# A graph-network kernel: 64-wide segment windows in one PSUM bank, edge values copied to PSUM by ScalarE, and another order of the last stretch

## The reference, cut to what matters

```python
# layer 0
h = gelu(x @ W_pre + b_pre)
aggr = segment_sum(h[src] * edge_attr, dst)
t = x + aggr
x = layernorm(x + t + gelu(gelu(t @ W1 + b1) @ W2 + b2))
# layer 1
norm = dinv[src] * dinv[dst]
agg = segment_sum((x @ W_lin.T + b_lin)[src] * norm[:, None], dst)
x = layernorm(x + relu(agg + x @ W_root.T + b_root))
```

## Time and profile before

| | us |
|---|---|
| median of three runs | 1217.83 (1215.64 to 1218.61) |
| the profiled execution | 1216.85 |
| its span, first to last instruction | 1215.0 |
| PE busy | 970.0 (80%) |
| POOL busy | 848.8 (70%) |
| DVE busy | 733.6 (60%) |
| ACT busy | 497.3 (41%) |

### The profile page before, as it was taken

The page is one execution under the profiler, slowest core; times in us unless marked ns, Lnnn a source line. Parts: engine busy times, 40 slices in busy tenths (PEclk is TensorE's granted clock), DMA queues, the critical chain, the costliest instruction groups (busy, mean ns, idle before and its releaser), DMA issues.

```text
span 1215.0 us, 21150 instructions
## 1 busy us (share of the span) xinstructions
PE 970.0 (80%) x7552; PEld 828.6 (68%) x7552; DVE 733.6 (60%) x1424; ACT 497.3 (41%) x820; POOL 848.8 (70%) x940
## 2 busy tenths in 40 slices
PE   6737677767768778879888989999999987996663
PEld 6635444434447557758767878899999986896553
DVE  8286867577765787676576676444455443543443
ACT  2305776565754676475655666300001000110032
POOL 7787777777777777777777777777777777760022
PEclk9767978687778889999999999999999997999766
DMA  8534776665657597888878988988888875878211
GB/s 222 160 107 130 260 234 227 195 222 179 232 188 223 184 318 250 259 263 258 274 247 283 294 291 283 311 260 231 245 228 243 222 207 148 255 189 200 70 48 42
DMA packets 195626, 263.62 MB, mean 217 GB/s; under 512 B 76828, under 2 KB 173084, under 8 KB 188540
## 3 DMA queue, kind: packets, MB, share of 16 engines
q1 hardware_dynamic: 167834, 218.28, 56.9%
q0 software_dynamic: 27392, 43.48, 14.4%
q10 hardware_dynamic: 290, 0.45, 0.1%
HBM read 175.10 MB, written 87.00 MB: 216 GB/s over the span
## 4 chain that ended last, share of the span: by engine, by line
PE 40%; POOL 32%; issue 12%; ACT 8%; DVE 5%; DMA 2%; SPq 1%; DVEq 0%; POOLq 0%; ACTq 0%
POOL gath L782 27%; PE bank_q L1393 24%; PE seg L1333 7%; ACT counts_raw L870 7%; PE bank_q L1364 5%; POOL gath L761 3%; PE bank_a L1293 1%; DMA gath<-table_h,srcs 1%; PE bank_q L1412 1%; DVE hots_raw L1236 1%; POOL counts_raw L769 1%; DVE bns L1067 1%; DVE stage L1062 1%; SPq L677 0%; DVE sumT L1259 0%
## 5 line engine op out<-in xcount | busy, mean ns | idle before, releaser
L782 POOL DMA_INDIRECT gath<-table_h,srcs x791 | 782.5, 989 | 241.1 <-issue 239.6
L870 ACT CAST counts_raw<-bank_q 128x490 bf16<-128x490 f32 x625 | 397.4, 698 | 248.1 <-PE bank_q L1364 245.5
L1393 PE MATMUL bank_q<-piece_raw,early_late 128*96 128x240 bf16 (+1 forms) x3807 | 423.7, 267 | 15.8 <-DMA piece_raw<-counts_hbm 12.3
L1393 PEld LDWEIGHTS bank_q<-piece_raw,early_late 128*96 128x96 bf16 x3807 | 396.6, 125 | 23.3 <-issue 14.3
L1364 PE MATMUL bank_q<-hots_raw 128*128 128x245 bf16 x1250 | 247.7, 295 | 122.6 <-ACT counts_raw L870 76.9
L1333 PE MATMUL seg<-onehot,msg 128*97 128x128 f32 x1662 | 242.9, 301 | 28.1 <-DVE msg L1159 21.1
L1364 PEld LDWEIGHTS bank_q<-hots_raw 128*128 128x128 bf16 x1250 | 99.7, 102 | 235.5 <-ACT counts_raw L870 162.9
L1333 PEld LDWEIGHTS seg<-onehot,msg 128*97 128x97 f32 x1662 | 222.0, 187 | 34.7 <-issue 23.0
L1236 DVE TENSOR_TENSOR hots_raw<-counters,kb 128x1960 bf16<-128x1960 bf16 (+1 forms) x157 | 182.4, 1162 | 0.0
L1159 DVE TENSOR_TENSOR msg<-gath,edg 128x480 f32<-128x480 f32 x166 | 108.2, 652 | 93.9 <-DMA gath<-table_h,srcs 88.8
L1234 DVE TENSOR_TENSOR hots_raw<-counters,kb 128x1024 bf16<-128x1024 bf16 (+1 forms) x157 | 107.0, 682 | 63.3 <-PE bank_q L1364 62.6
(11 more groups left out here) (158 smaller groups left out, 590.7 us busy)
## 6 DMA issues: line engine op xcount, KB each, us to landing
counts_hbm<-counts_raw SPq DMA_DIRECT2D x53, 1470.0 KB
piece_raw<-counts_hbm SPq DMA_DIRECT2D x260, 240.0 KB
edg<-in_edge SPq DMA_DIRECT2D x166, 240.0 KB, 4.1
gath<-table_h,srcs POOLq DMA_INDIRECT x791
piece_raw<-counts_hbm SPq DMA_DIRECT2D x62, 120.0 KB
piece_raw<-counts_hbm SPq DMA_DIRECT2D x26, 180.0 KB
table_h<-stage SPq DMA_DIRECT2D x12, 192.0 KB, 3.5
gath<-x_hbm SPq DMA_DIRECT2D x9, 240.0 KB, 4.7
```

The source lines that it names most:

```text
L782: pool.indirect_dma_start(gath[0:k, u % GS * UT + j, :], None, table[0], bass.IndirectOffsetOnAxis(ap=srcs[0:k, t:t + 1], axis=0)).then_in ...
L870: act.copy(counts[:, k % 2, :, i * 2 * WD:(i + 1) * 2 * WD].rearrange("p a (w n) -> p w a n", w=2), bank_q[m % 2][:, 0:2 * KC].rearrange(" ...
L1393: mm = pe.matmul(bank_q[bank_of(r)][0:D, 0:n], parts[:, FINE[c] + i, part, :], rows, start=(first and runs[r][3] is None and i == 0 and pa ...
```

## The change: what it does

1. **Edge values by way of PSUM.** ScalarE gets a new item `edges`: it copies a unit's edge values (128x480 fp32) from SBUF into a PSUM bank `edges`, one unit ahead, behind the product of the unit before. VectorE's product reads them there, behind a wait on that copy (`s_copied`). SyncE loads the next edge values behind the copy and not behind the product.
2. **Windows of 64, one bank.** `WIN` is 64 and not 128, so the one-hot has 320 columns and a matmul of `seg` 64. Each unit is its own group, so there are 167 adds of 64 columns and not 62 of 128. There is one bank `seg`, the other one became `edges`; TensorE's unit u waits for add u-1. (In these inputs a unit's destinations span at most 42 nodes.)
3. **Another plan.** `CREDIT` is (11, 17) and not (9.6, 15). The last node cuts take fewer units (`RATE` with 6 phases a unit at the end). From unit 162 on the pieces are placed by hand: 18 behind unit 163 beside those between phases, none behind units 164 and 165. Ahead of them `back` loads and the first `load`s stand behind one unit each from unit 159 on, and not all behind unit 166. `dense` items of the last cut are put ahead of phases 7 and 11.
4. **The final part.** From `at_end` on the runs rotate over five banks (three `bank_q`, `seg`, `edges`) and not three; the sets' transposes use two banks and not four. A set's phases stand 1, 2 and 5 spans behind its last span (`STEP_AT`) and not 0, 1 and 2.

Counted from the two lists (matmuls of pieces that stand behind the units of a range; the builds and pairs are the same in both):

| units | before | after |
|---|---|---|
| 50 to 109 | 1380 | 1488 |
| 110 to 119 | 435 | 507 |
| 120 to 149 | 1224 | 996 |
| 150 to 159 | 336 | 528 |
| 160 to 165 | 264 | 228 |
| behind unit 166 | 168 | 60 |

```diff
-GU = 3
-WIN = 128
+WIN = 64
+WIDE = 128
-CREDIT = (9.6, 15.0)
+CREDIT = (11.0, 17.0)
-BETWEEN = {0: 3, 1: 3, 3: 10, 8: 3}
+END = UNITS - 4
+BETWEEN = {1: 1, 3: 2, 8: 1}
+BEHIND = 18
+BETWEEN_LAST = {1: 1, 3: 3, 8: 2}
+STEP_AT = (1, 2, 2, 2, 5, 5, 5)
...
+            if i == 2:
+                order.append(("edges", u + 1))
...
+            def copy_edges(u):
+
+                act.wait_ge(s_edge[u % ES], edges_landed(u))
+                if u > 0:
+                    act.wait_ge(s_msg, u)
+                if u < UNITS:
+                    act.copy(edges[:, 0:UT * D], edg[:, u % ES].rearrange("p j d -> p (j d)")).then_inc(s_copied, 1)
...
-                dve.wait_ge(s_edge[u % ES], edges_landed(u))
+                dve.wait_ge(s_copied, u + 1)
...
                     dve.tensor_tensor(
                         msg[:, s, :, 0:D], gath[:, slot_tiles(u), :],
-                        edg[:, u % ES], ALU.mult).then_inc(s_msg, 1)
+                        by_tile(edges, UT), ALU.mult).then_inc(s_msg, 1)
...
-                if u == first_unit(g) and g >= 2:
-                    pe.wait_ge(s_add, g - 1)
+                if u >= 1:
+                    pe.wait_ge(s_add, u)
...
         def bank_of(r):
-            return 2 if r < one_bank else (r - one_bank) % 3
+            return 2 if r < one_bank else (r - one_bank) % 3 if r < at_end else (r - at_end) % 5
...
         def set_bank(c):
-            return (bank_a, bank_b, seg[0], seg[1])[c % 4]
+            return (bank_a, bank_b)[c % 2]
```

More of the change, by code:

```diff
@@ L185, in flush, with some @@
             order.append(("dense", waiting.pop(0)[1]))
+    def some(n, u, most):
+        for i in range(n):
+            if not open_run:
+                e = pick(ALL_UNITS + 6, 1)
+                if e is None:
+                    return
+                while len(waiting) > most:
+                    order.append(("dense", waiting.pop(0)[1]))
+                open_run.extend(begin(e, known))
+            emit_piece(u)
+    order.append(("edges", 0))
     for u in range(ALL_UNITS):
         order.append(("unit", u))
+        if u >= ALL_UNITS - GS:
+            order.append(("back", u - (ALL_UNITS - GS)))
+        if u >= ALL_UNITS - ES:
+            order.append(("load", LS_HOTS + u - (ALL_UNITS - ES)))
+        order += [("add", v) for v in range(ALL_UNITS) if added[v] == u]
         if u == META_AT:
             order.append(("meta", 0))
-        order += [("add", g) for g in range(GROUPS) if added[g] == u]
+        if u == END:
+            while open_run:
+                emit_piece(u - 1)
         flush(u)
@@ L220, in schedule @@
                     credit = min(credit, 2.0 * CT)
-    order += [("add", g) for g in range(GROUPS) if added[g] == ALL_UNITS]
-    order += [("load", f) for f in range(LS_HOTS, LS)] + [("back", c) for c in range(GS)]
+    order += [("add", v) for v in range(ALL_UNITS) if added[v] == ALL_UNITS]
+    order += [("load", f) for f in range(LS_HOTS + ES, LS)]
+    while open_run:
+        emit_piece(ALL_UNITS)
+    flush(2 * ALL_UNITS)
+    at_end = len(runs)
     for p, c in steps[ALL_UNITS]:
         order.append(("step0", p, c))
[L225 to L232, removed]
+        if c == CUTS - 1:
+            if p in (7, PHASES[0] - 1):
+                flush(2 * ALL_UNITS)
+            some(BETWEEN_LAST.get(p, 0), ALL_UNITS, 4)
         if p == PHASES[0] - 1:
@@ L237, in schedule @@
     flush(2 * ALL_UNITS)
-    late, done = [], 0
+    late, done = {}, 0
     for e in range(SPANS):
@@ L242, in schedule @@
             emit_piece(0)
-        order += [("last", e), ("dense", len(runs) - 1)]
-        order += late.pop(0) if late else []
+        order.append(("last", e))
+        order += [x for x in late.get(e, []) if x[1] == 0]
+        order.append(("dense", len(runs) - 1))
+        order += [x for x in late.pop(e, []) if x[1] != 0]
         while done < FINALS and min(SETS[done + 1] * P, N_NODES) <= span_end(e):
[L246 to L249, removed]
+            for p in range(PHASES[1]):
+                late.setdefault(e + STEP_AT[p], []).append(("step1", p, done))
             done += 1
-    for items in late:
-        order += items
-    return order, pieces, runs
+    for e in sorted(late):
+        order += late[e]
+    return order, pieces, runs, at_end
 def build(nc, x, xT_in, src, dst, first, tile_first, tile_rows, edge, edge_tail, W_pre, b_pre, W1, b1, W2, b2,
@@ L1392, in sum_piece @@
                     for part in range(3):
-                        mm = pe.matmul(bank_q[bank_of(r)][0:D, 0:n], parts[:, FINE[c] + i, part, :], rows,
+                        mm = pe.matmul(sums(r)[0:D, 0:n], parts[:, FINE[c] + i, part, :], rows,
                                        start=(first and runs[r][3] is None and i == 0 and part == 0),
```

180 lines of the change are left out of this document (93 added, 87 removed).

## The result

The changed kernel takes 1304.66 us, the kernel before 1218.22 on the same chip: ratio 1.0709, 95% interval 1.0682 to 1.0736. It is 7.1% slower, where 1152 us (5.4% faster) was forecast. The span of the profiled execution is 1304.3 us.

A forecast was written before the change was run, and what follows sets the result against it. GpSimd's gathers and TensorE were taken to set the end, then a tail of 125 us. 1215.0 less 19 (gathers), 5 (phase 0), 26 (last cut), 14 (spans) is 1150.6; with 1.85 outside, 1152 us; range 1140 to 1165.

The forecast's parts named there:

- the copy's place: ScalarE's copy behind the second pair: mostly covered by a TensorE piece, charged 0.15 us a unit (0 to 0.56).
- The other plan: Units 50 to 119: more piece matmuls, lag about 44 us at unit 110, 3 us of GpSimd waiting, gather end 1071.
- Phase 0 nearer to the last gather: Start of the last cut: phase 0 at 1080, 9 us behind the last gather (bounds 4 and 20), 14.4 before.
- The stalls beside products: Gathers lengthened beside products with both inputs in SBUF: 22.2 us among the 791 taken as gone.
- Product, windows, copy: Per unit: product unchanged in cost, ten segment matmuls 1.0 us (0.25 us less), a copy 0.56 us.
- Last cut and spans: The tail: last cut from 40.3 to 14 us, spans from 58.9 to 45 us.
- (a): Copy, product, segment sum and add tied through single banks: 6.86 us a unit, 1233 us in all; 5%.
- (b): Gathers: the product from PSUM still holds GpSimd, gather end 1090, 1167 us in all; 10%.
- (c): The tail only moves its waits: 12 us more for the last cut, 14 for the spans, 1178 us; 18%.
- (d): TensorE comes out late, a lower clock or the copies costing it 15 to 20 us: 1170 us; 15%.

The follow-up runs named there:

- e5: The changed kernel without the copy: VectorE's product reads edge values in SBUF again, one bank of sums kept; 1202.0 us against 1217.1 before, ratio 0.9905.
- e6: The changed kernel with the copy for unit u+1 moved to right behind unit u in ScalarE's queue; 1211.2 us, ratio 0.9940.
- e15: e5 with two banks in turn for the segment sums in place of one; 1196.5 us, ratio 0.9862.
- e18: e15 with the pieces handed out as before, CREDIT (9.6, 15.0) in place of (11.0, 17.0); 1169.1 us against 1219.2 before, ratio 0.9581.
- e14: e5 with windows of 128 in place of 64; 1206.9 us, ratio 0.9924.

## Why the prediction was wrong, step by step

**The step that failed: the copy's place.** "The copy stands behind the second pair, where TensorE has a piece of 1.2 us to do, so most of it is covered; I charge 0.15 us a unit (0 to 0.56 ...)". I priced the copy by its duration and not by its place. The duration was near (594 ns, forecast 560). What cost was that VectorE's product now waits for something that stands behind the evictions in another engine's queue, which depend on builds behind VectorE's own product. The working names what is queued behind the copy and whom that holds, but not what is queued ahead of it and who waits for the copy itself: the product. A unit was forecast 0.10 us longer; it took 7.83 us and not 6.63 (140.39 to 891.64; before, product 14 at 125.9 and product 110 at 762.20), of which 1.03 us went with the copy (e5: 6.80). The other wait, the copy's for the product before, was forecast as "met", and it was: 2.9 us from 103 to 900 us. The forecast looked at the wait that the copy makes, and not at the one that it causes. Shown by e6: the same copy in another place, 93 us less; and by e5: without it 103 us less.

**The other plan.** "I allow 3 us for GpSimd waiting (0 to 20)". Its own sum put the lag at unit 110 at "about 44, just where GpSimd has to wait" (30.8 and 60 units of 0.24 us make 45.2), and the allowance didn't take that seriously. Without the copy, e15 has a lag of 46.1 us at unit 104 already and its gathers end at 1109.0; e18 has 27.4 us and 1090.8: 18 us. The cost of more pieces was taken as their matmuls, 0.20 us a unit; TensorE's longer waits for builds, 19.5 us of 340 to 830, were left out.

**Phase 0 nearer to the last gather (9 us).** It came at 45.1 in the changed kernel, at 25.2 in e15 and 17.9 in e18; the kernel before had 14.4. "I take the earliest" was the mistake: matmuls behind unit 163 (12.96 us in one stretch from 1225.33) stand ahead of the products and segment sums of 164 and 165. VectorE's product of unit 164 starts only at 1237.20, 38 us behind the last gather's end. The rows separate two causes. From unit 160 to unit 164 the lag grows from 26.4 to 45.8 us in the changed kernel, from 7.7 to 26.6 in e15 and from 3.7 to 17.7 in e18, where before it stood at 5.6 and 4.5: 14 to 19 us of lag go with the pieces behind unit 163 in every kernel that has them there. The rest is what each kernel still lagged at unit 160, so the lag of the plan and of the ring isn't made up at the end.

**The stalls beside products** went as forecast: 958 ns and not 989, 24 us of gathers (forecast 22.2). Going through the whole trace in order of time, I find no gather lengthened beside a product (78 before, 22.7 us). With the product from SBUF, in e5, e15 and e18, it is 993, 992 and 990 ns again. The gain is real and was never collected: GpSimd waited for the products instead (155.8 us in the changed kernel, 53.0 in e6). A faster engine that runs ahead of a slower stream by a fixed depth gives back what it gains.

**Product, windows, copy:** 651 ns against 652, as forecast, and the PSUM operand costs VectorE nothing. By the Trainium skill, "VectorE: DVE Perf Modes", section on the TRN2 errata, it would by estimate have been 65 ns more (120 cycles of fixed part against 58); the trace doesn't agree (651 against 652 ns), and the measurement decides. Ten segment matmuls of 64 columns took 1.04 us from 1238.13, against 1.0 forecast, at a granted clock of 1.00 (2.4 GHz) from 1236 to 1240 us. In 110 to 340 us, at 0.52, they took 1.78 and 1.86 us (269.26, 275.43), which wasn't foreseen; in e5, at the same clock, no price of it shows. (The forecast's "0.3 us at best" for ten weight loads is a slip, since 1.25 less 0.81 is 0.44; nothing in the sum used it. The copy took 594 ns on average, 553 to 653.)

**Last cut and spans:** 11.5 and 36.1 us against 14 and 45, and in e18 11.6 and 34.8. The final part of the change does all that it was said to and more: 52 us of the tail gone. It is what carries e5, e15 and e18.

**The rivals.** (a), the ring, had the right kind of mechanism and 5%. It named the copy and the product among its members, but tied them by their single banks; what tied them was the copy's place behind the evictions. The bank of the sums is worth 0.4 to 0.9%, the copy in its place 8%. Its unit of 6.86 us was also too mild. (b) didn't happen; (c) didn't; (d) put 15 to 20 us on a lower clock or the copies' time, not on their place.

**Adding up**, over the medians where the kernel before takes 1217 to 1219 us: 1304.7 as changed; 1211.2 with the copy moved; 1202.0 without it; 1196.5 with two banks; 1169.1 with the pieces handed out as before. The 17 us from there to 1152 have about the size of the 19 us of gathers that the forecast counted and that a product from SBUF didn't have in e18; that is arithmetic, not a run. The medians come from several chips, on which those of the kernel before agree within 0.2%. Not tried, and so open: the copy in its early place, or two edge banks, with the lighter plan; the changed kernel as it is with the lighter plan alone; and the changed kernel with windows of 128.

## What to carry to other kernels

A helper operation put on a second engine has two prices: its duration, and its place in that engine's queue. Follow the consumer's wait back through everything that stands ahead of the helper; if that comes back to the consumer's own queue it is a ring, and the ring's time replaces the unit's time. And before loading more work on a stream that lags, ask whether the faster one has a cap: where your own sum lands on it, price the collision and not the average.

## What the hardware showed that was not expected

- The clock granted to TensorE from 110 to 340 us was 0.53 with segment matmuls of 64 columns and 0.81 with 128, in kernels alike but for that (e5, e14; e15, on e14's chip and with a second bank, also has 0.53); 0.52 to 0.57 in all five kernels with 64 of which the trace was read there (the changed one, e5, e6, e15, e18).
- An add of 0.22 us, behind a base index that VectorE reads into a register first, stood up to 1.4 us in "issue" where the product ahead of it came late (44.8 us over 108 times in the changed kernel, 2.8 us over 10 times in e5).
- On some chips every kernel took 1650 to 1730 us and not 1170 to 1305; the cause was not looked into.
